# A graph layer on one core: 14 destination tiles instead of 9 are summed through count matrices, and their 183 span bounds are searched in two passes

## What is computed

```python
xn = layernorm(x)
h_sparse = maxk(xn @ W_neigh, 32)                  # 32 largest of 256 kept per node
summed = segment_sum(h_sparse[src], dst, 6250)     # one 256-wide row added per edge
deg = segment_sum(ones, dst, 6250)
x = x + xn @ W_self + summed / max(deg, 1) + mix(xn)      # linear attention with a gate
x = x + ffn(layernorm(x))                          # on the 3124 rows of largest weight only
```

## Time and profile before

| | us |
|---|---|
| median of 3 runs | 2366.26 |
| the three runs | 2359.95, 2366.26, 2393.0 |
| the profiled execution | 2391.38 |
| its span (first to last instruction) | 2389.2 |
| first stage, 0 to 266 | 266 |
| aggregation, 266 to 2127 | 1861 |
| last stage, 2127 to 2389 | 262 |

### The profile page before, as it was taken

How to read it: one execution, slowest core, us unless ns; L and a number is a source line. 1 busy time by engine, 2 the same in 40 slices (tenths; PEclk the granted TensorE clock), 3 DMA queues, 4 the chain that set the end, 5 groups by cost and what they waited for, 6 DMA issues and landing times.

```text
span 2389.2 us, 29676 instructions
## 1 busy us (share of the span) xinstructions
PE 1505.8 (63%) x6995; PEld 945.6 (40%) x6995; DVE 1297.9 (54%) x4748; ACT 288.7 (12%) x764; POOL 1116.1 (47%) x1260
## 2 busy tenths in 40 slices
PE   2996545546655655765375666484748577653998
PEld 0553432223422422442243344352425354442666
DVE  6999624446754455555346546474555657475111
ACT  1443200000000000100001001011111111100211
POOL 2455646554656345445523644545353555342312
PEclk8998766667866776777677777786878677875999
DMA  8221333343433222323322322323232332231201
GB/s 172 67 77 60 111 91 102 84 112 95 124 86 96 65 78 85 90 65 87 91 64 75 95 80 79 100 76 89 72 91 78 88 111 72 81 91 47 71 18 29
DMA packets 128612, 199.87 MB, mean 84 GB/s; under 512 B 37596, under 2 KB 89643, under 8 KB 128510
## 3 DMA queue, kind: packets, MB, share of 16 engines
q0 software_dynamic: 53616, 131.54, 19.5%
q10 hardware_dynamic: 45176, 47.09, 7.3%
q1 hardware_dynamic: 29718, 20.03, 3.7%
HBM read 162.33 MB, written 35.71 MB: 83 GB/s over the span
## 4 chain that ended last, share of the span: by engine, by line
PE 30%; another core or an unknown queue 22%; DVE 21%; issue 18%; DVEq 3%; ACTq 2%; ACT 2%; SPq 1%; DMA 1%; POOL 0%; POOLq 0%
PE bank L1104 6%; DVE region_k L1462 5%; PE bank L1044 5%; DVE region_k L1461 5%; PE bank L1151 4%; PE bank L1165 3%; PE bank L1057 3%; PE bank L958 1%; PE bank L1030 1%; DVEq L1445 1%; ACTq L464 1%; DVE region_r L1346 1%; PE bank L1033 1%; DVE region_r L1342 1%
## 5 line engine op out<-in xcount | busy, mean ns | idle before, releaser
L719 POOL DMA_INDIRECT ring<-rows_d,stage x928 | 928.8, 1001 | 935.8 <-PE bank L1057 632.8
L1044 PE MATMUL bank<-region_k 128*125 128x500 f16 x978 | 407.9, 515 | 536.1 <-issue 216.8
L1461 DVE TENSOR_SCALAR region_k<-iota,region_k 128x125 f16<-128x125 f16 x978 | 281.6, 288 | 475.9 <-remote 408.2
L1044 PEld LDWEIGHTS bank<-region_k 128*125 128x125 f16 x978 | 156.8, 168 | 771.1 <-issue 352.0
L1462 DVE TENSOR_SCALAR region_k<-iota,region_k 128x500 f16<-128x500 f16 x978 | 350.9, 359 | 18.2 <-issue 17.8
L1057 PE MATMUL bank<-ring,region_v 128*125 x1084 | 315.2, 416 | 43.4 <-issue 43.3
L1445 DVE SCALAR_TENSOR_TENSOR region_v<-iota,tile_start,dstT 128x500 f16 x271 | 198.3, 740 | 77.6 <-issue 34.2
L874 ACT ACTIVATE region_k<-bank 125x500 f16<-125x500 f32 (+1 forms) x117 | 65.8, 578 | 1127.6 <-remote 852.6
L1057 PEld LDWEIGHTS bank<-ring,region_v 128*125 x1084 | 150.4, 139 | 126.8 <-issue 47.6
L1058 PE MATMUL bank<-ones,region_v 128*125 128x2 f16 x1084 | 182.4, 168 | 18.2 <-issue 17.7
L1058 PEld LDWEIGHTS bank<-ones,region_v 128*125 x1084 | 152.5, 141 | 29.7 <-issue 29.7
(11 more groups left out here) (307 smaller groups left out, 1988.8 us busy)
## 6 DMA issues: line engine op xcount, KB each, us to landing
ring<-rows_d,stage POOLq DMA_INDIRECT x928
kept_d<-region_v ACTq DMA_DIRECT2D x50, 252.0 KB
region_v<-xT_d ACTq DMA_DIRECT2D x53, 125.0 KB
xT_d<-region_r ACTq DMA_DIRECT2D x51, 125.0 KB, 2.0
rows_d<-region_r SPq DMA_DIRECT2D x50, 125.0 KB
region_k<-in_x_dram ACTq DMA_DIRECT2D x50, 125.0 KB
out_dram<-region_v ACTq DMA_DIRECT2D x50, 125.0 KB
region_v<-in_x_dram SPq DMA_DIRECT2D x5, 1120.0 KB
```

What stands on the lines that cost most here:

```text
L719: pool.indirect_dma_start(out=ring[:, c, :], out_offset=None, in_=rows_d, in_offset=bass.IndirectOffsetOnAxis(ap=stage[:, c:c + 1], axis=0 ...
L1044: m = pe.matmul(out, lo, key, start=(c == WINDOW_AT[unit.window]), stop=(c + 1 == WINDOW_AT[unit.window + 1]))
L1461: dve.tensor_scalar(lo, iota[:, 0:T], lo_staged[:, at, u:u + 1], None, ALU.is_equal)
```

## The change

ND goes from 9 to 14: tiles 9 to 13 are counted and summed densely instead of gathered. The planner now gives 182 windows, 1294 chunks and 191 units; five more dense positions (14) and five fewer gathered ones (36, of which 33 count). The rounds of gathers go from 29 to 24, so 768 gathers instead of 928. In `ORDER` the positions ahead of the fourteen dense ones count 7, 44, 21, 32, 39, 40, 4, 10, 4, 64, 30, 28, 28 and 28 chunks. Counting positions have 39 chunks on average, between 4 and 86, and up to 13 units.

NEDGE becomes 183, over the 128 partitions, so the comparison runs twice, on 128 and on 55 edges: four more comparisons, one more copy, one more small reduction on DVE, and two more one-column or one-row matmuls. `last_row` and `win_below` have 128 columns and partitions.

```diff
-    ND = 9
+    ND = 14
+    EDGES = [range(first, min(first + 128, NEDGE)) for first in range(0, NEDGE, 128)]
...
-                pe.matmul(bank[(5, 7, 2, 3)[q]][0:NEDGE, 0:CH // 4], last_row[:, 0:NEDGE], dstT[:, first:first + CH // 4],
+                pe.matmul(bank[(5, 7, 2, 3)[q]][:, 0:CH // 4], last_row[:, :], dstT[:, first:first + CH // 4],
                           start=True, stop=True)
...
+            for e, edges in enumerate(EDGES):
+                m = pe.matmul(bank[6][0:1, 128 + edges.start:128 + edges.stop], bcol[0:len(edges), 1 + e:2 + e],
+                              ident[0:len(edges), 0:len(edges)], start=True, stop=True)
...
-            found = []
-            for q in range(4):
-                if q >= 2:
-                    st.after(found[q - 2])
-                found.append(st.mark(dve.tensor_scalar(win_below[:, q % 2, :], bank[(5, 7, 2, 3)[q]][0:NEDGE, 0:CH // 4], small[0:NEDGE, 4:5], 0.0,
-                                              ALU.is_lt, ALU.add, accum_out=bcol[0:NEDGE, 2 + q:3 + q])))
+            found, parts = [], 1 + len(EDGES)
+            for e, edges in enumerate(EDGES):
+                held = len(edges)
+                for q in range(4):
+                    if len(found) >= 2:
+                        st.after(found[-2])
+                    at = parts + 4 * e + q
+                    found.append(st.mark(dve.tensor_scalar(win_below[0:held, q % 2, :], bank[(5, 7, 2, 3)[q]][0:held, 0:CH // 4],
+                                                           edge_col[0:held, e:e + 1], 0.0, ALU.is_lt, ALU.add,
+                                                           accum_out=bcol[0:held, at:at + 1])))
```

More of the change, by code:

```diff
@@ L163, in build @@
     NEDGE = ND * NW + 1
+    EDGES = [range(first, min(first + 128, NEDGE)) for first in range(0, NEDGE, 128)]
+    assert len(EDGES) == 2
     with ExitStack() as ctx:
@@ L287, in build @@
         region_r.at, after_ek = ek_at, region_r.at
-        win_below = region_r.take([NEDGE, 2, CH // 4])
+        win_below = region_r.take([128, 2, CH // 4])
         row_b = region_r.take([1, NT + 1])
@@ L323, in build @@
         below = region_r.take([NT + 1, NG])
-        last_row = region_r.take([128, max(NT + 1, NEDGE)])
+        last_row = region_r.take([128, 128])
         wg1 = region_r.take([128, KC, GH])
@@ L361, in build @@
         tile_edge = sb("tile_edge", [NT + 1, 1])
-        bcol = sb("bcol", [max(NT + 1, NEDGE), 6])
+        bcol = sb("bcol", [128, 2 + 5 * len(EDGES)])
+        edge_col = sb("edge_col", [128, len(EDGES)])
         bn6 = sb("bn6", [T, 6])
@@ L927, in _ @@
                 first = GC + q * (CH // 4)
-                pe.matmul(bank[(5, 7, 2, 3)[q]][0:NEDGE, 0:CH // 4], last_row[:, 0:NEDGE], dstT[:, first:first + CH // 4],
+                pe.matmul(bank[(5, 7, 2, 3)[q]][:, 0:CH // 4], last_row[:, :], dstT[:, first:first + CH // 4],
                           start=True, stop=True)
-            pe.matmul(bank[6][0:NEDGE, 0:1], edge_row.rearrange("p a b -> p (a b)")[:, 0:NEDGE], ones[0:1, 0:1],
-                      start=True, stop=True).then_inc(s_edge_sums, 1)
+            for e, edges in enumerate(EDGES):
+                m = pe.matmul(bank[6][0:len(edges), 8 + e:9 + e], edge_row.rearrange("p a b -> p (a b)")[:, edges.start:edges.stop],
+                              ones[0:1, 0:1], start=True, stop=True)
+            m.then_inc(s_edge_sums, 1)
             pe.wait_ge(s_bcol, 1)
             pe.matmul(bank[6][0:1, 64:64 + NT + 1], bcol[0:NT + 1, 0:1], ident[0:NT + 1, 0:NT + 1], start=True, stop=True)
-            pe.matmul(bank[6][0:1, 128:128 + NEDGE], bcol[0:NEDGE, 1:2], ident[0:NEDGE, 0:NEDGE], start=True, stop=True)\
-              .then_inc(s_edge_sums, 1)
+            for e, edges in enumerate(EDGES):
+                m = pe.matmul(bank[6][0:1, 128 + edges.start:128 + edges.stop], bcol[0:len(edges), 1 + e:2 + e],
+                              ident[0:len(edges), 0:len(edges)], start=True, stop=True)
+            m.then_inc(s_edge_sums, 1)
             turn(0, 0)
@@ L1207, in _ @@
                 if b == 0:
-                    dve.tensor_scalar(last_row, ones[:, 0:max(NT + 1, NEDGE)], ident[:, 127:128], None, ALU.mult).then_inc(s_lastrow, 1)
+                    dve.tensor_scalar(last_row, ones[:, :], ident[:, 127:128], None, ALU.mult).then_inc(s_lastrow, 1)
             row_stats(3)
@@ L1215, in _ @@
             dve.tensor_scalar(below, bank[4][0:NT + 1, 0:NG], tile_edge[:, 0:1], None, ALU.is_lt)
-            b = st.mark(dve.tensor_copy(small[0:NEDGE, 4:5], bank[6][0:NEDGE, 0:1]))
+            for e, edges in enumerate(EDGES):
+                b = st.mark(dve.tensor_copy(edge_col[0:len(edges), e:e + 1], bank[6][0:len(edges), 8 + e:9 + e]))
             st.after(b)
-            found = []
-            for q in range(4):
-                if q >= 2:
-                    st.after(found[q - 2])
-                found.append(st.mark(dve.tensor_scalar(win_below[:, q % 2, :], bank[(5, 7, 2, 3)[q]][0:NEDGE, 0:CH // 4], small[0:NEDGE, 4:5], 0.0,
-                                              ALU.is_lt, ALU.add, accum_out=bcol[0:NEDGE, 2 + q:3 + q])))
+            found, parts = [], 1 + len(EDGES)
+            for e, edges in enumerate(EDGES):
+                held = len(edges)
[6 more added lines that the diff above has]
+                                                           accum_out=bcol[0:held, at:at + 1])))
             st.after(found[-1])
-            dve.tensor_reduce(bcol[0:NT + 1, 0:1], below, AX_X, ALU.add)
-            dve.tensor_reduce(bcol[0:NEDGE, 1:2], bcol[0:NEDGE, 2:6], AX_X, ALU.add).then_inc(s_bcol, 1)
+            for e, edges in enumerate(EDGES):
+                dve.tensor_reduce(bcol[0:len(edges), 1 + e:2 + e], bcol[0:len(edges), parts + 4 * e:parts + 4 * e + 4], AX_X, ALU.add)
+            dve.tensor_reduce(bcol[0:NT + 1, 0:1], below, AX_X, ALU.add).then_inc(s_bcol, 1)
             row_stats(4)
```

## The result

| | before | after |
|---|---|---|
| time, us (median) | 2369.6 (4 runs, 2360 to 2393) | 2447.9 (4 runs, 2445 to 2452) |
| ratio | 1 | 1.035, 95% interval 1.030 to 1.040 |
| span of the profiled execution | 2389.2 | 2444.8 |
| first stage, to the first gather | 266.1 | 285.9 |
| aggregation | 1863.3 | 1895.8 |

The changed kernel is 3.5% slower, by 78 us between the medians. The profiled execution of before was slow among its own, so the two traces differ by 56 us only: 20 in the first stage, 32 in the aggregation, 3 in the last. (The aggregation is measured here from the first gather to the last matmul of its last position; the prediction's window ended 2 us earlier.)

The account below looks back on a forecast made before the run. It took POOL's gather runs, each followed by a serial tail of POOL idleness, as the bound; -210 - 22 + 95 + 113 + 2.5 = -21.5 us, applied to the median 2366, gave 2345 us, range 2270 to 2440.

Parts of the forecast that it names:

- Gathers: POOL's runs in the aggregation: 160 fewer gathers at 1.31 us each, all off the path, -210 us.
- Tails: POOL idle after gather runs: five fewer gathered cycles -22, 316 more chunks at 0.30 us +95, five more dense positions +113.
- The prediction's own test: Cycles with 60 or more chunks: tails of 22 us and more say slope 0.30, above 27 0.45, under 17 0.17.
- Search: Search of bounds on DVE ahead of the first stage: four comparisons, one copy, one small reduction, nothing hiding them, +2.5 us.
- Last stage: The stage after the aggregation: the change hardly touches it, so no term in the sum.
- The steep slope: Counting in the aggregation: each chunk wholly in the tail at 0.45 us, sum +44 us, 2410 us.
- Rival 2: Between a run's last gather and the next freed slot: everything added is exposed, +110 us, 2476 us; chance 0.22.
- Rival 1: Counting hides inside the gather runs: slope 0.17, dense positions stay at 19 us, -95 us, 2271 us; chance 0.31.
- Rival 3: More DVE one-hots put all 768 gathers at the slow pace, 0.07 us over the mean: +54, 2399 us; chance 0.06.
- Dense matmuls at half clock: Dense positions: matmuls with a row mean well above 441 ns would put up to 12 us on each of 14.
- the late updates: While gathers are issued, PE's semaphore updates arrive late; ACT waits 852.6 us on "remote", DVE 408.2.

Follow-up runs that it names:

- e3: Changed kernel with PE signalling a freed one-hot slot once in four chunks instead of after every chunk; ratio 1.0316 to the kernel before.
- e4: Kernel before with PE signalling a freed one-hot slot once in four chunks instead of after every chunk; ratio 1.0095.
- e1: Kernel before with 14 increments of an unused semaphore at DVE's start, moving its loop on; ratio 1.0114.
- e2: Changed kernel with 60 increments of an unused semaphore at DVE's start, moving its loop on; ratio 1.0216 to the kernel before.
- e12: Kernel before with POOL waiting, after every second group of gathers, until the group just issued has landed; ratio 1.1544.

## Why the prediction was wrong

Forecast 2345 us, range 2270 to 2440; measured 2448. Against the profiled execution of before the sum was -21.5 us, and the traces differ by +55.6. The 77 us between them are, by term:

- **Gathers, -210: right.** 768 at 1.316 us in their runs (1.28 to 1.36 said).
- **Tails, -22 + 95 + 113 = +186: the step that failed, and in it the price of a chunk.** Counted as the prediction counts them, the tails rose by 242 us, so 56 too little was put down, and POOL's waits rose to 884 us where 810 to 850 were said. With the other two terms as they stand, the 316 chunks cost 0.48 us each and not 0.30. A straight line through the tails, without the first two cycles, gives 0.30 us a chunk in the kernel before, so the prediction read its slope rightly, and 0.48 in the changed kernel, where a dense position costs 24 us (18 before). With those two cycles, which are unlike the others (no counting in one, 48 or 114 chunks under 56 or 80 gathers in the other), it is 0.13 and 0.31, and 16 and 20 us for a dense position: steeper by 0.18 as well. The prediction's own test says nearly the same: the cycles with 60 chunks and more and no dense position, 60, 63, 66 and 86, have tails of 25.6, 26.8, 28.7 and 37.2 us ("above 27 say 0.45"), and the one with 64 chunks and a dense position 54.5. What it had wrong is that a slope of before would hold. Its cycles of before all had nearly the same cover, and two windows, which PE can fill before it must wait for a copy, held 12 to 40 chunks there. The change adds chunks, and it takes away the long runs in which they hid (13 before, 4 after) and makes the windows short. That these two are what raised the price is read from the timelines and the counts of chunks; no run changed the windows or the number of count banks alone, so their shares stay open.
- **Search, +2.5: right in itself, but 17 us of branch stall** came with it, which no row of before shows.
- **Last stage, 0:** +3.2, not looked into.

56 + 17 + 3 = 76, and the rest is rounding. Another 23 us of the distance between the medians come from the profiled execution of before, which took 2391 us against a median of 2370; the prediction allowed for that and applied its difference to the median.

**The steep slope**, 0.45, kept as an end of the range, is the best of the sums: without the search it gives +41 us for the aggregation, where +32.5 was measured. **Rival 2** (everything added is exposed) had the place and the reason (two windows are 10 chunks where they were 12 to 40; the runs after 1489 us mostly hide 10 to 15), and I gave it 0.22. Its 2476 is nearer to 2448 than the forecast is, but partly by luck: for the aggregation it says +107, 75 us too much, where the forecast's -24 is 57 too little. The branch stall and the 23 us between the medians, which are in neither sum, make up the difference. What spoke against it, five tails not on one line, was scatter between cycles and no evidence of cover. **Rival 1** (the counting hides) falls with the slope. **Rival 3** (dearer gathers) falls on the first chip, where a gather takes 0.996 us against 1.001. On the other chips, where DVE goes on making one-hots during the runs, it is there: 1.072 us a gather with fourteen tiles against 1.050 with nine, 17 us in 768. The rule of the Trainium skill that the prediction cites with it, from "SBUF — State Buffer", section "SBUF: two separate sides", agrees in sign, and again as a stretch, not as a full block. **Dense matmuls at half clock** did not come (426 ns against 441); the 12 us each that the prediction gives them is worked out from no row.

What the experiments add is that a loss does not need the late updates, on which the prediction built its picture. On chips without them the change loses more, 6.6%. There both engines' chain of counting is next to the bound already (1202 us of 1332), so that the removed gathers bring back 67 us of 210, against 168 for the added work. On the 2400 kind I have no experiment that puts a number on the late updates' part. That they expose the counting there rests on the timelines, on the time from a window's last matmul to its copy, and on the difference between the chips, about 540 us of tails in either kernel (599 against 59, and 885 against 349).

## What to carry to other kernels

Work taken off the engine that sets the pace is worth its time only while it is the only one near the bound: run the kernel with most of that work left out, and the distance to the full kernel is all that leaving it out can win (131 us of 1861 for 696 gathers, on the chips where this was run). A slope read off cycles holds for the cover that these cycles had; here the same line gave 0.30 us a chunk before and 0.48 after. When a change adds work and takes away what it hides under, work the sum out at the fully exposed price too, and look for what was hidden and comes out. And put a few idle instructions ahead of a long loop before believing a loss of one per cent: the stall was 17 of 2448 us.

## What the runs showed of the hardware

- The same kernel takes 2370 to 2425 us on two chips and 1858 to 1863 on four others. Of the difference of the profiled executions, 530 us, 531 are in the aggregation (1863 against 1332), while the first and the last stage are alike to 2 us. Gathers are not slower on the 2400 kind (0.993 us on average from 350 to 1500 us, 1.049 on the other). DVE's busy time is the same (993 us), PE's 48 us longer, at a granted clock of 0.74 against 0.87, so slower work is a small part. What differs is that semaphore updates of PE seldom get through while POOL issues gathers one after another: 28% fall inside a gather at 51% of the time, against 72% at 74% on the other kind, and in the changed kernel 22% at 43%, against 65% at 58%. For 45% of PE's signals no update is recorded within 1 us (31% in the changed kernel; 0.3% or less on the other kind). In the first 5 us of a run it is 42%, from 5 to 10 us 90%, and in the tails almost none. DVE's updates are held back much less: for 10% of them none is recorded within 1 us, and where 38% of its updates fall inside a gather, 46% of its signalling instructions end there (69 and 70% on the other kind). Why, the runs do not tell; fewer signals did not help (e3, e4).
- A loop body of 296 DVE instructions costs nothing or 3.7 to 4.5 us a round extra, by 14 instructions ahead of it (e1) and 60 (e2).
- When POOL, right after it issued the last of a group's four gathers, waits until the group has landed, it waits 3.5 us on average (407.3 us over 116, e12).
